# A causal attention row prepared in smaller pieces: other steps for the next row's normalisation, projections and loads, in a four-layer kernel on one core

## The reference

```python
qkv = x @ Wqkv_w + Wqkv_b                      # 16 heads of 8
scores = q @ k^T * scale + causal_mask
y_softmax = softmax(scores) @ v
# a matrix state per head, run over the positions
state = retention * state + Gamma * (v_t k_t^T);   y_t = (W_static + state) q_t
alpha = sigmoid(gelu(x @ gate_w1 + gate_b1) @ gate_w2 + gate_b2)
y = alpha * y_softmax + (1 - alpha) * y_stp
return y @ out_w + out_b
```

## Time and profile before

| what | value |
|---|---|
| median of 3 runs | 1957.99 us (1957.63 to 1964.93) |
| the profiled execution, own time | 1961.1 us |
| its span, first to last instruction | 1959.7 us |
| mean granted TensorE clock | 0.929 |
| PE, DVE, ACT, POOL busy | 86%, 66%, 57%, 35% |
| row 1, 2, 3, 4 of the causal part (first exponential to the next row's first) | 165.3, 167.2, 167.3, 137.7 us |

### The profile page before, as it was taken

How to read it: one execution, slowest core, us unless ns; L and a number is a source line. 1 busy time by engine, 2 the same in 40 slices (tenths; PEclk the granted TensorE clock), 3 DMA queues, 4 the chain that set the end, 5 groups by cost and what they waited for, 6 DMA issues and landing times.

```text
span 1959.7 us, 45111 instructions
## 1 busy us (share of the span) xinstructions
PE 1680.7 (86%) x19451; PEld 1030.4 (53%) x19472; DVE 1287.2 (66%) x2063; ACT 1117.2 (57%) x1713; POOL 694.6 (35%) x508
## 2 busy tenths in 40 slices
PE   4588889999999999999976778878877888799999
PEld 2355656777677677767752232423423342366665
DVE  5565746666666666766667678667766876665664
ACT  3264576767666776677641567556656766633221
POOL 5221203442344244324451444454444454411100
PEclk7798999999999999999995789988978998899999
DMA  7655000000000000000134263135226222100000
GB/s 176 178 157 133 6 14 1 2 2 2 1 2 2 1 2 2 2 2 1 39 115 83 71 152 82 45 110 135 60 87 152 66 66 64 26 6 7 11 11 12
DMA packets 38359, 102.07 MB, mean 52 GB/s; under 512 B 3856, under 2 KB 12176, under 8 KB 34704
## 3 DMA queue, kind: packets, MB, share of 16 engines
q1 hardware_dynamic: 38160, 99.18, 19.7%
HBM read 66.93 MB, written 31.46 MB: 50 GB/s over the span
## 4 chain that ended last, share of the span: by engine, by line
PE 53%; DVE 22%; issue 7%; ACT 5%; POOL 4%; DMA 1%; POOLq 0%; SPq 0%; DVEq 0%; ACTq 0%
DVE arena L1394 7%; PE accs L1299 5%; PE ring L2110 3%; PE accs L2548 3%; PE accs L2174 3%; PE ring L2526 3%; PE ring L2528 3%; PE ring L2136 3%; DVE arena L1404 3%; PE ring L1274 2%; PE ring L1248 2%; PE ring L2104 2%; PE ring L1842 2%; POOL xn L290 2%; PE ring L2116 1%
## 5 line engine op out<-in xcount | busy, mean ns | idle before, releaser
L1394 DVE TENSOR_REDUCE arena<-ring 128x2 f32<-128x1024 f32 (+2 forms) x320 | 344.4, 1111 | 128.6 <-PE ring L1255 70.2
L1482 ACT ACTIVATE arena<-ring 128x1024 f32<-128x1024 f32 (+3 forms) x384 | 297.8, 808 | 137.3 <-PE ring L1281 100.8
L1248 PE MATMUL ring<-arena 48*128 48x512 bf16 (+3 forms) x768 | 141.0, 376 | 59.2 <-DVE arena L1394 15.6
L1274 PE MATMUL ring<-arena 51*128 51x512 bf16 (+3 forms) x768 | 133.4, 361 | 62.8 <-DVE arena L1394 45.6
L1299 PE MATMUL accs<-arena 128*9 128x512 f32 (+3 forms) x1536 | 180.4, 545 | 3.7 <-ACT arena L1482 3.6
L2404 POOL TENSOR_TENSOR arena<-arena 128x1280 f32<-128x1280 f32 x28 | 65.3, 2332 | 266.5 <-PE accs L2174 235.1
L2388 POOL TENSOR_TENSOR arena<-arena 128x1024 f32<-128x1024 f32 x32 | 76.0, 2376 | 199.7 <-DVE arena L2264 199.7
L2396 POOL TENSOR_TENSOR arena<-arena 128x512 f32<-128x512 f32 x112 | 141.8, 1299 | 11.3 <-DVE arena L2245 11.3
L290 POOL TENSOR_SCALAR xn<-x,moments,rstd 128x128 f32<-128x128 f32 x88 | 70.6, 816 | 197.1 <-DVE rstd L261 192.3
L2671 ACT ACTIVATE arena<-ring 128x512 f32<-128x512 f32 x80 | 47.7, 597 | 147.2 <-PE ring L2526 140.5
L1638 POOL TENSOR_TENSOR arena<-arena 128x1024 f32<-128x1024 f32 x28 | 65.8, 2351 | 171.2 <-ACT arena L1495 133.6
(11 more groups left out here) (347 smaller groups left out, 4286.8 us busy)
## 6 DMA issues: line engine op xcount, KB each, us to landing
arena<-whole_k SPq DMA_DIRECT2D x32, 512.0 KB, 4.6
arena<-whole_q SPq DMA_DIRECT2D x32, 512.0 KB, 6.2
arena<-a_scratch_q SPq DMA_DIRECT2D x16, 384.0 KB, 6.6
arena<-a_scratch_k SPq DMA_DIRECT2D x16, 384.0 KB, 9.1
arena<-c_scratch_q SPq DMA_DIRECT2D x16, 384.0 KB, 8.9
arena<-c_scratch_k SPq DMA_DIRECT2D x16, 384.0 KB, 10.7
a_scratch_k<-arena SPq DMA_DIRECT2D x8, 512.0 KB, 4.1
c_scratch_k<-arena SPq DMA_DIRECT2D x8, 512.0 KB, 5.8
```

The source lines that it names most:

```text
L1248: mm = nc.tensor.matmul(o[r], qs[half(r, SCORE), pair, n * P:(n + 1) * P], ks[half(r, SCORE), pair, a:c], start=True, stop=not diag)
L1274: mm = nc.tensor.matmul(ps[:, r * BANK:r * BANK + cols], ks[half(r, SHIFT), pair, j * P:(j + 1) * P], qs[half(r, SHIFT), pair, a:a + cols] ...
L1394: nc.vector.tensor_reduce(dst, src, AX.X, ALU.max, negate=True).then_inc(c_max_taken.up(item), 1)
L1482: nc.scalar.activation(view(c_probs[wi % 4]), view(ps), ACT.Exp).then_inc(c_weights_made.up(item), 1)
```

## The change

It does the following.

1. For the next row, the statistics are 4 items of 2 tiles each, at steps 7 to 10. Log and root move to 11 and 12, the turns from 11 and 12 to 14 and 16. q moves from step 13 to 17, k from 17 to 21, the v halves from 14 and 16 to 18 and 20, gate1 from 18 to 22, gate2 from 21 to 25. The second bf16 part of q and k moves from 15 and 19 to 19 and 23, the writes from 16 and 20 to 20 and 24, and the loads of the stacks from 21 and 23 to 25 and 27.
2. POOL makes the first 4 normalised tiles at the root item, and the second 4 (and the bias) at the first turn.
3. The ring buffer of q and k is given free after ACT's first copy (c_full); the second copy reads c_full instead of PSUM.
4. scale and read of a round stand one step later (except in round 7).
5. In the last row the expert layer's items move a little: statistics, log, root and first turn one step earlier, logits and exp too; first, rest, next, weigh and split are spread and later, rows goes from step 43 to 47.
6. The planner's TIMES follow.

```diff
             elif kind in ("q", "k"):
-                pe.wait_ge(c_split, (kind, b, "high"))
+                pe.wait_ge(c_full_made, (kind, b))
...
-                nc.scalar.activation(c_parts[:, 0, :], ps[:, :], ACT.Identity, bias=bias, scale=scale).then_inc(
-                    c_split.up((kind, b, "high")), 1)
+                ac.wait_ge(c_full_made, (kind, b))
+                nc.scalar.activation(c_parts[:, 0, :], c_full[:, :], ACT.Copy).then_inc(c_split.up((kind, b, "high")), 1)
...
-            prepare = lambda b: [[("norm", b)], [("log", b)], [("root", b)], [("turn", b, 0)], [("turn", b, 1)], [("q", b)],
-                                 [("v", b, 0)], [("mid", b, "q")], [("write", b, "q"), ("v", b, 1)], [("k", b)], [("gate1", b)],
-                                 [("mid", b, "k")], [("write", b, "k")], [("gate2", b), *loads(b, 0)], [], loads(b, 1)]
+            prepare = lambda b: {
+                7: [("stats", b, 0)], 8: [("stats", b, 1)], 9: [("stats", b, 2)], 10: [("stats", b, 3)], 11: [("log", b)],
+                12: [("root", b)], 14: [("turn", b, 0)], 16: [("turn", b, 1)], 17: [("q", b)], 18: [("v", b, 0)],
+                19: [("mid", b, "q")], 20: [("write", b, "q"), ("v", b, 1)], 21: [("k", b)], 22: [("gate1", b)],
+                23: [("mid", b, "k")], 24: [("write", b, "k")], 25: [("gate2", b), *loads(b, 0)], 27: loads(b, 1)}
...
-                    side[s + 4 + (j == 0)].append(("scale", b, j))
-                    side[s + 5].append(("read", b, j))
+                    more = j < HD - 1
+                    side[s + 4 + more].append(("scale", b, j))
+                    side[s + 5 + more].append(("read", b, j))
...
-            TIMES = {"turn": (1.1, (("A", 0.6),), 1), "q": (2.0, (("A", 2.2),), 1), "k": (2.0, (("A", 2.2),), 1),
+            TIMES = {"turn": (1.1, (("A", 0.6),), 1), "q": (2.0, (("A", 1.1),), 1), "k": (2.0, (("A", 1.1),), 1),
...
-                        dve_norm_stats(s, item[1])
+                        dve_norm_stats(s, b, 2 * i, 2 * i + 2)
...
-                    elif kind == "turn":
-                        _, b, h = item
-                        pool_norm_tiles(s, b, h)
-                        if h == HALVES - 1:
-                            add_bias(b)
+                    elif kind == "root":
+                        pool_norm_tiles(s, item[1], 0)
+                    elif kind == "turn" and item[2] == 0:
+                        pool_norm_tiles(s, item[1], 1)
+                        add_bias(item[1])
...
-            8: [("clear",), ("stats", 0, 0)], 9: [("stats", 0, 1)], 10: [("stats", 0, 2)], 11: [("stats", 0, 3)], 12: [("log", 0)],
-            13: [("root", 0)], 15: [("turn", 0, 0)], 16: [("turn", 0, 1)], 33: [("logits", 0)], 35: [("exp", 0)],
-            36: [("share", 0)], 37: [("top", 0), ("first", 0)], 38: [("rest", 0), ("next", 0)], 39: [("weigh", 0)],
-            40: [("split", 0, 0)], 41: [("split", 0, 1)], 43: [("rows", 0)]}
+            7: [("clear",), ("stats", 0, 0)], 8: [("stats", 0, 1)], 9: [("stats", 0, 2)], 10: [("stats", 0, 3)], 11: [("log", 0)],
+            12: [("root", 0)], 14: [("turn", 0, 0)], 16: [("turn", 0, 1)], 32: [("logits", 0)], 34: [("exp", 0)],
+            36: [("share", 0)], 37: [("top", 0)], 38: [("first", 0)], 40: [("rest", 0)], 41: [("next", 0), ("weigh", 0)],
+            42: [("split", 0, 0)], 43: [("split", 0, 1)], 47: [("rows", 0)]}
```

15 lines of the change are left out of this document (9 added, 6 removed), and 2 rows, old and new, of the table TIMES.

## The result

The changed kernel takes **2017.6 us** (median of 4 runs, 2012.6 to 2019.5) against 1958.6 for the kernel before, measured beside it: ratio 1.029, 95% interval 1.026 to 1.032. It is slower, as forecast, but by 59 us and not by 21.6; its time lies above the range. The profiled execution took 2017.2.

What follows compares the result with a forecast made beforehand. It took TensorE, busy 86% of the span, to be held by waits in the next row's preparation. Three rows at +8.2 (+24.6) and −3 for the last gave +21.6 on the 1958.0 median: 1979.6 us, range 1950 to 2001.

Steps and rivals of the forecast that it cites:

- The wait for the stack half at step 25 as the main loss: Step 25, rows 1 to 3: PE waits about 16 us for the next row's stack half; per row +8.2 us.
- k's end 56: Row's preparation: k's projection ends 56 us behind step 9's exponential, before T + 46.6; may be 4 us off either way.
- PE at the maxima tile, T + 70: Step 25: PE reaches the maxima tile needing the stack half 14 us behind k's end, 70 us behind step 9's exponential.
- From k's end to the landing, 30: Split, writes, fetches and loads of k: 28 to 32.5 us, taken as 30, before 28.6; stack half lands at T + 86.
- gate2 behind the wait, 0.9: Behind step 25's wait: gate2, with as many matmuls as a value half but narrower, takes 0.9 us.
- Scale and read later, zero or 2 either way: Each row's scale and read a step later: zero cost, at most 2 us either way in a row.
- Second turn not early: Preparation's second turn: its four tiles don't come early on POOL; PE arrives some 5 us earlier, its wait stays as long.
- Release at the first copy, 1.1 us for each of q and k: Ring buffer of q and k: earlier release saves about 1.1 us for each, contained in the 88% busy rate.
- The last row, −3: Last row: ACT idle and the rows item's wait go, root ends later; net −3 us, ends −7 and +2.
- Rival 1: Load chain short enough, so only removed waits count: 26 us faster, 1932 us; chance 0.10.
- Rival 2: Stack-half wait gives back just the gain, k's end at T + 50 and chain 28: 1955 to 1966 us; chance 0.18.
- Rival 3: k's second copy waits for q's landing, half clock slows PE: each row +14, 1997 to 2001 us; chance 0.10.

## Why the prediction was right in sign and wrong in size

The runs give an account, each part on top of the one above (medians of different batches):

| kernel | us | row 2 |
|---|---|---|
| before | 1958.6 | 167.2 |
| + statistics in four items | 1951.8 | 162.8 |
| + early tiles | 1937.0 | 160.4 |
| + scale and read later | 1955.5 | 167.3 |
| + release at first copy, new last row | 1951.1 | 167.3 |
| + later steps: the change | 2017.6 | 187.5 |

The later steps cost 66 us on top of the rest, but 48 when put into the 1937.0 us kernel, which has neither later scale and read nor the release nor the new last row. How the 18 us between them divide is open, but the traces show what differs. Step 16 takes 9.8, 10.8 and 9.8 us in the three rows of the change and 5.1, 5.8 and 5.7 with the later steps alone: only where read too is a step later does it stand between root's tiles and the second turn's. Steps 21 and 22 give more than that back, 11.4 us in row 2 against 18.1, since k then doesn't wait for q's landing. And with the later steps alone the first maxima tile comes behind gate2, which is done ahead of the wait at full clock; in the change it comes ahead of gate2, and putting gate2 ahead took 20 us off.

Point by point, row 2, behind step 9's exponential (T = 1278.2):

- *The wait for the stack half at step 25 as the main loss*: right. The wait is 19.06 us and stands in all three rows at 18.7 to 19.6; bringing the loads forward halves it, and with gate2 early and the tile held to step 28 as well it is under 2 us.
- *Root's end, T + 12, and the second turn, T + 28*: T + 14.5 and T + 30.4. *q's end 35.5, k's end 56*: 37.3 and 57.1. *PE at the maxima tile, T + 70*: T + 72. All 1 to 2.5 us late, in the bounds.
- *From k's end to the landing, 30*: 34.1. **This is the first term that was mis-sized.** Up to the third part it took 11.9 where I had 13.1 to 15.4. But the loads landed 14.6 us behind their issue for the last one, and I took 7.3 to 9.6 from the earlier trace rows, from a stretch where no fetch was right ahead of them, though I had named the megabyte. With the loads ahead of the fetch the last one lands 7.8 us behind its issue and the chain is 24.1; the parts of k had landed by T + 72.9 in both.
- *gate2 behind the wait, 0.9*: **the second.** From landing to step 26's exponential it took 6.6 us where before 1.7 lay between: a weighing of 1.89, then gate2 with 3.17 for fourteen matmuls, all at half clock. I had put the half clock into a rival and not into the term. And I had taken gate2 for as many matmuls as a value half. The rows have sixteen for gate2 and eight for a value half: even at full clock it is 1.96 us. So step 26 starts at T + 97.9 (before T + 80.4): +17.5 where the sum had +8.2.
- *Scale and read later, zero or 2 either way*: **the third.** The runs give 18.5 us alone, and in the change 10 with round 0's scale a step too early, some 30 by the estimate without that. I looked for slack at the scan; the cost stands at steps 44 and 45, where beta (eight transpositions on PE) waits for the tile that POOL makes for it behind a later read and kv (2.32 us; the two steps take 13.1 and not 8.6), and between step 9 and step 26, 2 to 2.5 us a row in the 1937.0 us kernel.
- *Second turn not early*: right. The wait of 5.48 us ahead of it ends with DVE's reduction behind the scan, which itself waits 4.74 for kv. By the rule cited in the prediction (the Trainium skill, "SBUF — State Buffer", section "SBUF: two separate sides") one of VectorE and GpSimd blocks while the other holds their shared ports. The trace agrees: in the change the four tiles take 5.18 us beside the scan, one of them 2.86 and the others 0.79 each, and seven take 5.44 without a scan.
- *Release at the first copy, 1.1 us for each of q and k*: not found in the kernel before (1.003, 1.000 to 1.007). With the later steps and the old release PE waits 12.5 us for ACT's second copy (L963) in front of score tiles, which itself waits for q's landing. But the release doesn't save that either: in the change with scale and read put back, which has the new release and the same wait for q, steps 21 and 22 take 17.6 us against 18.1. No run shows a gain from it.
- *The last row, −3*: −4.3, in its bounds.
- *Rival 1* (chain short enough) fell. *Rival 2* asked for k's end at T + 50; it came at 57.1. *Rival 3*, k's second copy waiting for q, showed 0.56 us in the change (and 2.5 to 2.9 in three other kernels, where k comes earlier); its half clock was real, though not set off by the wait.

Counted up for row 2: from 8.2 to 17.5 by the landing and what is behind it, 3.7 more behind step 26, less 0.8 at its start, makes 20.3 to 20.4. Three rows make 55.9 of span, the 1.4 us ahead of the first and the last row's −4.3 included.

Open: the release and the last row come to −4.5 us in the account, no more than those runs differ (1930 to 1959 for one kernel), though the last row alone is worth 9 elsewhere. In those ten executions the time falls as the mean granted clock rises, 0.950 in the fastest and 0.932 in the slowest, and in the traces the first exponential stands anywhere from 1061.9 to 1071.4 us, though nothing ahead of it differs between the kernels but the release of q's and k's buffer. What sets clock and spread wasn't found.

## What to carry to other kernels

Moving a producer in a fixed order of items without its consumer is priced by the whole chain, and the chain's length is not fixed: look behind which transfer of another stream the loads fall in the queue, since k two steps later cost nothing, and the whole preparation later, with k by four steps, cost 48 us. Price what stands right behind a long wait at the clock that such a stretch had in the trace, and count its matmuls there. And where several small moves are made at once, try each alone: two of these gained 21 us at their old steps, and the others gave back nearly four times that.

## What the runs showed of the hardware

The four loads of k of 384 KB each took a median of 9.6 us to land without a fetch right ahead and 16.7 behind one megabyte of fetch, the DMA engines busy for 0.83 of that stretch. Not all of it is the fetch: in the change q's loads went out 1 us ahead of k's and not 4 to 5. The last load of k's first half landed 7.8 us behind its issue with the loads ahead of the fetch and q's 4 us ahead, 10.6 with no fetch ahead but q's 1.6 us ahead (the kernel with k two steps later), and 14.6 in the change. TensorE was granted 0.50 over the whole of step 25, from 5 us ahead of the wait on; there fourteen matmuls of gate2 took 3.17 us. In the 1937.0 us kernel, at a granted clock of 1.00, they took this:

```profile
1306.98 1.73 PE L1217 MATMUL ring<-weights_small,arena 64*128 64x16 f32 x14
```

That ratio, 1.83 for the same fourteen matmuls, is nearly that of the two levels, 1.2 and 2.4 GHz. The low clock doesn't need the wait: with the tile held to step 28, gate2 took 2.90 us where no long wait stood ahead of it, at a granted clock of 0.55.
